# New constants for the order planner of a Mamba-2 plus routed-attention kernel

## The chip, the cores and the metric

The kernel runs on one core of one Trainium2 chip. The metric is the device time of one execution in microseconds. Three executions of the kernel before took 3627.47, 3632.01 and 3639.0 us, with a median of 3632.01 us.

## The reference

The input is `x`, 8 sequences of 1024 tokens with 512 features. After a layer norm it goes two ways, and both results are added to `x`:

```
xn = layernorm(x)
# way 1, Mamba-2: d_inner 1024, state 128, 16 heads of 64
u  = layernorm(xn) * ln_w + ln_b
z, xBC, dt = split(u @ in_proj_w.T)
xBC = silu(causal_conv4(xBC) + conv_b);  dt = softplus(dt + dt_bias)
y  = selective scan over the 1024 tokens with exp(-exp(A_log) * dt)
y  = (y + D * xs) * silu(z);  y = y / rms(y) * gamma
way1 = xn + y @ out_proj_w.T
# way 2, for each of 4 groups g and 8 sequences b: routed attention
queries    = top 512 tokens of xn @ w_qr[g]
key_values = top 256 tokens of xn @ w_kvr[g]
q = queries @ w_q[g].T;  k, v = split(key_values @ w_kv[g].T)   # 8 heads of 64
v = v * sigmoid(key/value logit);  one null key and null value join them
o = softmax(q k^T / 8) v;  o = (o @ w_out[g].T) * sigmoid(query logit)
way2 = mean of o over the groups that took the token, null_token where none did
out  = x + way1 + way2
```

Products are computed to nearly single precision by splitting each factor into a high and a low half-precision part, so that a product is three matrix multiplications.

## The kernel before

**Two halves.** The first half is the Mamba way. It runs over 16 blocks of 512 tokens, each of 4 chunks of 128 tokens. In it, `turn` is a DMA that transposes a normed chunk into `xhT` (L2287), and `gate` is a DMA that transposes the gated result of a chunk into `yT` (L2293), from which `proj` multiplies by the output weights (L1275). Between the halves the top tokens are found by a search over 32 bits.

The second half is the attention. It runs over 32 items, one for each group and sequence. An item has these parts on TensorE:

- *prepare*: `q` (4 steps of 12 matmuls, L1314), `k` (2 steps, L1329), `v` (2 steps, L1343). They read `xq` and `xk`, which 6 transposing DMAs `row` (L2371) fill from 6 gathers.
- *maxima*: `max` (16 steps, L1359), each followed on VectorE by `max_out` (L1826 and L1827), which takes the row maximum; then `shift_turn` (L1367) and `null_turn` (L1375).
- *heads*: `score` (8 steps, L1389 and L1390) and `value` (8 steps, L1406 to L1410). Between them ScalarE takes the exponential (`soft`, L2100) and its high half (`high_p`, L2106); GpSimd (`low_p`, L2238) and VectorE (`low_v`, L1861) each make half of the low part. After `value`, VectorE divides (`norm_o`, L1867 and L1870), ScalarE and GpSimd split the result (`o_high` L2112, `o_low` L2243).
- *finish*: two transposing DMAs `oturn` (L2394) fill `oT`, and `out` (4 steps of 12 matmuls, L1421) multiplies by the output weights. ScalarE scales (`res`, L2119) and GpSimd adds the rows to the output by an indirect DMA (`store`, L2232).

Each engine executes its instructions in a fixed order and waits on semaphores. SP issues all DMAs other than the indirect and the adding ones, so a DMA that waits holds back every later one on that queue. `rank` (L1764) is a VectorE step that counts places for the gathers of a later item.

**The planner.** The order is worked out in Python when the kernel is built, and it is the same in every execution. It is made in two stages.

1. `weave` (L188) writes a rough line of TensorE steps. The heads of item n are the main thread. At share s of it, a `Part(feed, start, end)` (L180) has been brought to the share `start + s * (end - start)` of its own steps. Beside the heads of item n lie prepare(n+1), maxima(n+1) and finish(n-1) (L847 to L851). `HEAD_START` (L49) is a pause ahead of the heads.
2. `Order` (L197) runs a model of the five engines over that line. Each step has an engine, a duration, the steps that it waits for, the PSUM banks that it takes with the steps that give them back, and `extra`, a time from the end of its issue to its result (for DMAs the landing). When TensorE is free, the model goes through the first `ahead` steps still in the line, takes the first one of each kind, and starts the first of those that has its inputs and banks (L294). The other engines start the ready step with the earliest latest-start (`latest`, L221). That time comes from the steps that follow; for a step that gives a bank back it is also no later than its matmul's end plus `keep` (L234).

The times that the model reaches are used only to sort the steps into each engine's order and to choose the banks. The instructions, their sizes and their waits are not touched by any constant of the planner, except which step's bank a matmul waits for.

`AHEAD_M` and no `keep` are used for the Mamba half (`arrange`, L434), `AHEAD` and `KEEP` for the attention (`arrange_items`, L611).

Of the kernel before, what the change touches and what calls it, by code (L numbers as in the profile page):

```python
# [38 lines left out]

FIRST_SLICES = 12  # L40
SLOP = 0.7
KEEP = 4.0
AHEAD, AHEAD_M = 12, 4
TURNS = CK * 3.45 + 15.23
TURN_ISSUE, TURN_LANDS, GATE_LANDS = 0.6, 4.0, 5.0
CONV_START, CONV_END = -0.05, 1.05
AHEAD_1, CONV_START_1 = (-0.06, 3.64), -0.25
BEHIND = 2
HEAD_START = 1.0  # L49
NSLOT = 4  # L50
ROW_ISSUE, ROW_LANDS = 0.6, 4.0
O_ISSUE, O_LANDS = 0.6, 5.0
NW = 4 * D
SC = 128
NSP = NW // SC
# [141 lines left out]
class Order:  # L197
# [13 lines left out]
    def add(self, engine, us, step, after=(), seats=(), extra=0.0):  # L211

        self.nodes[step] = (engine, us, [a for a in after if a], seats, extra)
        if engine == "PE":
            self.line.append(step)
# [229 lines left out]
def arrange_steps(order, line, late):  # L445
# [3 lines left out]
    def last(step):  # L449
        return step if step[1] >= 0 else None  # L450
# [85 lines left out]
    for ch in range(NCH):  # L536
        i = ch // CK
        add("SP", 0.5, ("bc_in", ch), [("cum_store", i), last(("intra", ch - 2)), last(("bc_in", ch - 1))], extra=10.0)
        free = [] if ch < 2 or ends(ch - 2) else [("xw", ch - 2)] if opens(ch - 2) else [("xw", ch - 2), ("decayed", ch - 2)]
        add("DVE", 0.25, ("dec_arg", ch), [("bc_in", ch), ("cum_copy", i)] + free)  # L540
        add("ACT", 0.45, ("dec", ch), [("dec_arg", ch)])
        for k in range(4):
            add("ACT", 1.26, (f"diff{k}", ch), [("dec", ch)])
        add("ACT", 1.91, ("decay", ch), [(f"diff{k}", ch) for k in range(4)])
        add("DVE", 0.28, ("gram_out", ch), [("gram", ch), last(("mask", ch - 1))])
        add("DVE", 2.6, ("mask", ch), [("decay", ch), ("gram_out", ch)])
        add("ACT", 0.25, ("open_b", ch), [("open", ch), state_before(ch)])
        add("DVE", 1.22, ("xdt", ch), [("open", ch), ("bias_get", len(PIECES) - 1), ("slice_low", len(PIECES) - 1), last(("intra", ch - 1))] + ([] if ends(ch - 1) else [("xw", ch - 1)]))
        add("DVE", 1.22, ("dxs", ch), [("open", ch), ("xdt", ch), ("bias_get", len(PIECES) - 1), ("slice_low", len(PIECES) - 1), last(("y2" if opens(ch - 1) else "y_skip", ch - 1))])
        if not ends(ch):  # L550
            add("POOL", 2.0, ("xw", ch), [("xdt", ch), ("dec", ch), state_before(ch)])
            if not opens(ch):
                add("POOL", 2.5, ("decayed", ch), [("dec", ch), ("state_out", ch - 1)] + ([] if opens(ch - 1) else [("inter", ch - 1)]))
                add("DVE", 1.22, ("state_out", ch), [("state", ch), ("decayed", ch), ("inter", ch)])
            else:
                add("DVE", 1.22, ("state_out", ch), [("state", ch), last(("inter", ch - 1))])
        for j in range(2):
            add("ACT", 0.59, ("z_tanh", ch, j), [("z", ch, j), ("wout_low", KI - 1), last(("yz", ch - 1))])
            add("DVE", 0.69, ("z_silu", ch, j), [("z_tanh", ch, j)])
        if opens(ch):  # L560
            add("DVE", 1.22, ("y2", ch), [("intra", ch), ("dxs", ch), ("wout_low", KI - 1), last(("y_low", ch - 1))])
        else:
            add("DVE", 1.22, ("y_in", ch), [("inter", ch), ("cum_exp", i), ("y_low", ch - 1)])
            add("POOL", 2.7, ("y_skip", ch), [("y_in", ch), ("dxs", ch)])
            add("DVE", 1.22, ("y2", ch), [("intra", ch), ("y_skip", ch)])
        add("DVE", 1.23, ("yz", ch), [("y2", ch), ("z_silu", ch, 0), ("z_silu", ch, 1)])
        add("ACT", 1.2, ("square", ch), [("yz", ch), last(("gate", ch - 1))])
        add("DVE", 0.2, ("mean", ch), [("square", ch)])
        add("POOL", 0.8, ("root", ch), [("mean", ch)])
        add("ACT", 1.15, ("y_high", ch), [("root", ch)])  # L570
        add("DVE", 1.4, ("y_low", ch), [("y_high", ch)])
        add("SP", TURN_ISSUE, ("gate", ch), [("y_low", ch), last(("proj", ch - 1))], extra=GATE_LANDS)
        add("ACT", 0.58, ("proj_out", ch), [("proj", ch), last(("o_add", ch - 2))])
        add("POOL", 1.0, ("o_add", ch), [("proj_out", ch), ("skip_store", i)], extra=5.0)
    if not late:
        return
    blk = NBLK - 1
    for h in range(2):
        add("DVE", 0.65, ("rank_get", h), [("rank_in", h), ("skip_store", blk)])
    for bit in range(31, -1, -1):  # L580
        add("DVE", 1.7, ("bit", bit), [("bit", bit + 1) if bit < 31 else ("rank_get", 1)])
    add("DVE", 0.9, ("ranks_zero", 0), [("inter", CK * blk - 1)])
# [28 lines left out]
def arrange_items(plan, line):  # L611
# [57 lines left out]
    for n in range(ITEMS):  # L669
        if n:  # L670
            for j in range(RT):
                if j in (0, QT):
                    add("SP", 0.5, ("rank_load", n, j // QT), [("rank", n, j - 1) if j else ("slot", n - 1)], extra=3.5)
                add("DVE", 1.05, ("rank", n, j), [("rank_load", n, j // QT), ("rank", n, j - 1) if j else ("slot", n - 1)])
            add("DVE", 0.2, ("slot", n), [("rank", n, RT - 1)] + each("store", n - NSLOT, QT) + each("qscore", n - 2, QT) + each("gather", n - 4, RT))
            for j in range(RT):
                add("POOL", 1.05, ("gather", n, j), [("slot", n), ("row", n - 1, RT - 1 if j >= QT else QT - 1)] + ([("row_score", n - 1, j)] if j >= QT else []), extra=4.0)
                read = ("q", n - 1, KD - 1) if j < QT else ("v", n - 1, KT - 1)
                add("SP", ROW_ISSUE, ("row", n, j), [("gather", n, j), read], extra=ROW_LANDS)
                if j >= QT:  # L680
                    add("DVE", 0.1, ("row_score", n, j), [("gather", n, j), ("v_low", n - 1, KT - 1)])
# [13 lines left out]
        if n % NB < 2:  # L695
            add("DVE", 1.2, ("keys_null", n), [("nulls", n // NB), ("max", n - 2, QT * H // 2 - 1)] + ([("keys_id", 1)] if n == 1 else []))
        for k in range(QT * H // 2):
            add("DVE", 0.84, ("max_out", n, k), [("max", n, k)] + [("null_arg", n - 1)])
        add("DVE", 0.3, ("shift", n), each("max_out", n, QT * H // 2) + [("shift_turn", n - 1), ("null_split", n - 1)])
        add("DVE", 0.25, ("null_arg", n), [("shift", n)])  # L700
        add("DVE", 0.42, ("shift_out", n), [("shift_turn", n), ("shift_in", n - 1)])
# [4 lines left out]
        for h in range(H):  # L706
            add("ACT", 1.05, ("soft", n, h), [("score", n, h), back_by("low_p", n, h, 2), back_by("low_v", n, h, 2)])
            add("ACT", 1.05, ("high_p", n, h), [("soft", n, h), back_by("value", n, h, LAG + 1)])
            add("POOL", 1.2, ("low_p", n, h), [("high_p", n, h)])
            add("DVE", 1.0, ("low_v", n, h), [("high_p", n, h)])  # L710
            add("DVE", 0.66, ("norm_o", n, h), [("value", n, h), back_by("o_low", n, h, 2)])
            add("ACT", 0.42, ("o_high", n, h), [("norm_o", n, h)] + each("oturn", n - 1, QT // 2))
            add("POOL", 0.7, ("o_low", n, h), [("o_high", n, h)])
# [10 lines left out]
def make_plan():  # L724
# [119 lines left out]
    for n in range(ITEMS):  # L844
        others = []
        if n + 1 < ITEMS:
            others.append(Part(Feed(prepare(n + 1), 20.8, record), 0.2, 2.0))  # L847
            others.append(Part(Feed(maxima(n + 1), 10.2, record), -0.7, 1.1))
        if n:
            others.append(Part(Feed(finish(n - 1), 10.4, record), -0.7, 1.2))  # L850
        weave(Feed(heads(n), HEAD_START + H * 1.8, record), *others)  # L851
    for gen in (last_values(), finish(ITEMS - 1)):
        Feed(gen, 1, record).to(1)
# [1615 lines left out]
```

## Time and profile before

| | us |
|---|---|
| median of three executions | 3632.01 |
| the profiled execution | 3642.05 |
| its span, first to last instruction | 3640.7 |
| TensorE busy | 3360.3 (92%) |
| VectorE busy | 2962.7 (81%) |
| ScalarE busy | 2273.6 (62%) |
| GpSimd busy | 1850.6 (51%) |

The mean granted clock of TensorE was 0.968 of full speed. Busy shares are means over the whole span; a busy time of TensorE is of pipelined matmuls, so an end-to-start overlap is counted once. A wait is put down to the engine whose signal came last.

### The profile page before, as it was taken

To read this page: it belongs to the slowest core of one execution; us is meant where nothing else is said; L and a number is where in the kernel's file an instruction comes from. 1 tells how busy PE (TensorE), PEld (TensorE's weight loads), DVE (VectorE), ACT (ScalarE), POOL (GpSimd) and SP (SyncE) were. 2 spreads that over 40 slices of the span, in tenths; PEclk is the share of its full clock that TensorE was granted. 3 is DMA by queue.
4 is the path that set the end of the run, shared out by engine and by line. 5 is a ranking of instruction groups with operands and counts; after the bars stand their busy time and mean duration, and the time that the engine had idled before them with its cause. 6 is when DMAs were issued, how large, how long until landed. Compare 5 with 4: busy or idle time off the path is not lost.

```text
span 3640.7 us, 64398 instructions
## 1 busy us (share of the span) xinstructions
PE 3360.3 (92%) x24312; PEld 1940.5 (53%) x24312; DVE 2962.7 (81%) x5336; ACT 2273.6 (62%) x4329; POOL 1850.6 (51%) x1483
## 2 busy tenths in 40 slices
PE   6899999999999999999748999999999999999997
PEld 4455555555555555555424555555555555555554
DVE  6798989999898988989967777787787877787774
ACT  5767767677767666776426555566555755555564
POOL 1332433334343332323437888877665765666565
PEclk9899999999999999999868999999999999999998
DMA  5444544465554445444387576777676676577664
GB/s 160 94 109 112 114 94 102 102 128 114 116 120 81 102 114 116 116 103 84 77 127 158 101 131 119 127 147 151 120 141 128 146 133 125 115 133 136 126 113 68
DMA packets 834213, 428.02 MB, mean 118 GB/s; under 512 B 575239, under 2 KB 758663, under 8 KB 831856
## 3 DMA queue, kind: packets, MB, share of 16 engines
q1 hardware_dynamic: 777584, 320.97, 42.5%
q0 software_dynamic: 56320, 102.94, 15.9%
q8 instruction: 193, 3.16, 0.4%
q14 instruction: 116, 0.95, 0.1%
HBM read 176.19 MB, written 101.71 MB: 76 GB/s over the span
## 4 chain that ended last, share of the span: by engine, by line
PE 58%; DVE 14%; DMA 8%; issue 5%; POOL 5%; ACT 4%; SPq 1%; another core or an unknown queue 0%; POOLq 0%; ACTq 0%; DVEq 0%
PE pair L1314 7%; PE pair L1275 7%; PE pair L1197 7%; PE pair L1421 7%; PE pair L1245 6%; PE pair L1285 4%; PE pair L1329 3%; DMA oT<-ohl 2%; PE pair L1343 2%; PE pair L1389 2%; PE pair L1390 2%; PE pair L1359 2%; PE pair L1256 2%; PE pair L1265 2%; DMA de<-cum 2%
## 5 line engine op out<-in xcount | busy, mean ns | idle before, releaser
L2238 POOL TENSOR_TENSOR ph<-pf,ph 128x512 f16<-128x512 f32 x256 | 354.8, 1386 | 243.8 <-ACT ph L2106 241.6
L1571 DVE SCALAR_TENSOR_TENSOR cv<-raw,taps,cv 128x512 f32<-128x512 f32 x480 | 428.6, 919 | 29.1 <-ACT cv L1978 27.9
L1826 DVE TENSOR_REDUCE smx<-pair 128x2 f32<-128x514 f32 x512 | 349.7, 684 | 88.3 <-PE pair L1359 85.5
L1197 PE MATMUL pair<-xhT,whi 128*128 128x512 f16 x1280 | 385.5, 383 | 8.1 <-ACT btok L1998 2.1
L2100 ACT ACTIVATE pf<-pair 128x1024 f32<-128x1024 f32 x256 | 261.6, 1023 | 155.0 <-PE pair L1390 131.8
L1275 PE MATMUL pair<-ohi,yT 128*128 128x512 f16 x1024 | 319.8, 384 | 27.1 <-DMA yT<-yhl 25.8
L1245 PE MATMUL pair<-zhi,xhT 128*128 128x512 f16 x1024 | 326.2, 380 | 1.5 <-ACT btok L1998 1.2
L1861 DVE TENSOR_TENSOR ph<-pf,ph 128x512 f16<-128x512 f32 x256 | 254.8, 995 | 84.3 <-ACT ph L2106 81.3
L2008 ACT ACTIVATE de<-de,cum 128x128 f32<-128x128 f32 x1024 | 309.5, 388 | 1.2
L2106 ACT CAST ph<-pf 128x1024 f16<-128x1024 f32 x256 | 267.3, 1044 | 4.9 <-PE pair L1410 0.2
L1285 PEld LDWEIGHTS pair<-xdt,de 128*128 128x128 f32 x2048 | 244.7, 196 | 20.4 <-issue 12.5
L2232 POOL DMA_INDIRECT y<-res,slot_i x128 | 208.4, 1628 | 84.9 <-ACT res L2119 65.9
L1285 PE MATMUL pair<-xdt,de 128*128 128x64 f32 x2048 | 242.7, 278 | 6.9 <-DVE dxs L1607 6.9
L2243 POOL TENSOR_TENSOR ohl<-of,ohl 128x256 f16<-128x256 f32 x256 | 202.8, 808 | 83.7 <-ACT ohl L2112 81.9
L1197 PE MATMUL pair<-xhT,wlo 128*128 128x512 f16 x640 | 245.1, 383 | 0.0
L1408 PE MATMUL pair<-vhi,ph 128*128 128x65 f16 x2048 | 243.8, 196 | 0.5 <-issue 0.5
L1410 PE MATMUL pair<-vhi,ph 128*128 128x65 f16 x2048 | 243.7, 195 | 0.3 <-issue 0.3
L1409 PE MATMUL pair<-vlo,ph 128*128 128x64 f16 x2048 | 243.3, 195 | 0.0
L2211 POOL DMA_INDIRECT gat<-rows,slot_i x192 | 197.4, 1028 | 55.6 <-issue 32.7
L1406 PE MATMUL pair<-nvb,pnT 96*128 96x65 f16 x1024 | 202.3, 198 | 21.3 <-issue 6.7
L2172 POOL TENSOR_TENSOR yn<-yn,neghalf 128x1 f32<-128x1 f32 x64 | 49.1, 767 | 335.4 <-DVE yn L1661 335.2
L1197 PEld LDWEIGHTS pair<-xhT,whi 128*128 128x128 f16 x1280 | 124.1, 99 | 169.6 <-issue 36.3
(260 smaller groups left out, 9811.6 us busy)
## 6 DMA issues: line engine op xcount, KB each, us to landing
de<-cum SPq DMA_DIRECT2D x64, 1024.0 KB, 9.4
rows<-rowt SPq DMA_DIRECT2D x16, 1040.0 KB, 6.2
xin<-x SPq DMA_DIRECT2D x16, 1024.0 KB, 8.8
y<-xin SPq DMA_DIRECT2D x16, 1024.0 KB, 5.7
y<-ob POOLq DMA_DIRECT2D x64, 256.0 KB, 4.6
qb<-qa SPq DMA_DIRECT2D x32, 512.0 KB
rbc<-rank SPq DMA_DIRECT2D x63, 256.0 KB
wst<-wkv SPq DMA_DIRECT2D x32, 256.0 KB
```

The source lines that it names most:

```text
L1197: ins = pe.matmul(bk[:], w[:, k, ws], xt[:, ha, k, :], start=n == 0, stop=n == 3 * KD - 1)
L1245: pe.matmul(pz[:], xt[:, ha, k, cs], w[:, k, j * 512:(j + 1) * 512], start=n == 0, stop=False)
L1275: ins = pe.matmul(bk[:], yT[:, ha * KI + k, :], w[:, k, :], start=k == 0 and n == 0, stop=k == KI - 1 and n == 2)
L1285: ins = pe.matmul(pw[:, h * HD:(h + 1) * HD], de[ch % 2][:, h, :], xdt[:, h, :], start=True, stop=True)
L1314: ins = pe.matmul(bk[:], w[:, k, ws], xq[:, ha * KD + k, :], start=n_ == 0, stop=n_ == 3 * KD - 1)
L1421: ins = pe.matmul(bk[:], o_[:, ha * KD + k, :], w[:, k, :], start=k == 0 and m == 0, stop=k == KD - 1 and m == 2)
L1571: ve.scalar_tensor_tensor(c_[:], r_[:, t:t + BLK], taps[:, ct, t:t + 1], c_[:], ALU.mult, ALU.add).then_inc(done, 1)
L1826: ve.tensor_reduce(smx[:, qt, 2 * h2:2 * h2 + 2], sc[:, :, 0:NK + 1], AX.X, ALU.max)
L2008: ins = ac.activation(d_[:, h, :], d_[:, h, :], ACT.Relu, bias=cum_t[i % 2][:, c, h:h + 1], scale=-1.0)
L2100: ac.activation(f[:].rearrange("p k q -> p (k q)"), bank("score", n, h)[:], ACT.Exp, scale=SCALE).then_inc(S.pf, 1)
L2106: ac.copy(p_[:, 0], f[:]).then_inc(S.ph, 1)
L2238: po.tensor_tensor(p_[:, 1, 1], f[:, 1], p_[:, 0, 1], ALU.subtract).then_inc(S.plp, 1)
```

## The change

No instruction is added or taken away. Constants of the planner change, and one dependency of its model is added. The durations and landing times that the model gives to the four kinds of transposing DMAs become longer in issue and shorter in landing. Three VectorE durations (`rank`, `max_out`, `low_v`) become shorter. `KEEP` goes from 4 to 6, `AHEAD` from 12 to 24, `HEAD_START` from 1.0 to 0.5, and the three parts beside the heads get other starts and ends. `TURN_ISSUE`, `TURN_LANDS`, `GATE_ISSUE` and `GATE_LANDS` are used in the Mamba half; all others act on the attention, `ROW_...` also on the first rows at the end of the Mamba half. `rank_get` 1 is now ordered behind `rank_get` 0.

```diff
-KEEP = 4.0
-AHEAD, AHEAD_M = 12, 4
+KEEP = 6.0
+AHEAD, AHEAD_M = 24, 4
-TURN_ISSUE, TURN_LANDS, GATE_LANDS = 0.6, 4.0, 5.0
+TURN_ISSUE, TURN_LANDS = 1.3, 2.5
+GATE_ISSUE, GATE_LANDS = 1.9, 2.9
-HEAD_START = 1.0
+HEAD_START = 0.5
-ROW_ISSUE, ROW_LANDS = 0.6, 4.0
-O_ISSUE, O_LANDS = 0.6, 5.0
+ROW_ISSUE, ROW_LANDS = 1.3, 2.7
+O_ISSUE, O_LANDS = 2.9, 2.6
...
-        add("SP", TURN_ISSUE, ("gate", ch), [("y_low", ch), last(("proj", ch - 1))], extra=GATE_LANDS)
+        add("SP", GATE_ISSUE, ("gate", ch), [("y_low", ch), last(("proj", ch - 1))], extra=GATE_LANDS)
...
-        add("DVE", 0.65, ("rank_get", h), [("rank_in", h), ("skip_store", blk)])
+        add("DVE", 0.65, ("rank_get", h), [("rank_in", h), ("skip_store", blk)] + ([("rank_get", h - 1)] if h else []))
...
-                add("DVE", 1.05, ("rank", n, j), ...
+                add("DVE", 0.95, ("rank", n, j), ...
-            add("DVE", 0.84, ("max_out", n, k), ...
+            add("DVE", 0.7, ("max_out", n, k), ...
-            add("DVE", 1.0, ("low_v", n, h), [("high_p", n, h)])
+            add("DVE", 0.85, ("low_v", n, h), [("high_p", n, h)])
...
-            others.append(Part(Feed(prepare(n + 1), 20.8, record), 0.2, 2.0))
-            others.append(Part(Feed(maxima(n + 1), 10.2, record), -0.7, 1.1))
+            others.append(Part(Feed(prepare(n + 1), 20.8, record), 0.1, 1.8))
+            others.append(Part(Feed(maxima(n + 1), 10.2, record), -0.5, 1.1))
         if n:
-            others.append(Part(Feed(finish(n - 1), 10.4, record), -0.7, 1.2))
+            others.append(Part(Feed(finish(n - 1), 10.4, record), -1.0, 1.3))
```

## Rows read from the trace of the kernel before

**Rows 1.** Busy time by stretch: length, engines, TensorE clock, DMA share, GB/s.
```profile
150.00:1740.00 1590.00, 1543.90 (x8620) 873.01 (x8619) 1429.27 (x1987) 1121.10 (x2569) 569.93 (x360) 0.99 0.49 107
1740.00:1900.00 160.00, 92.59 (x430) 50.72 (x430) 123.67 (x222) 55.16 (x107) 57.16 (x46) 0.76 0.58 94
1926.00:3582.00 1656.00, 1561.08 (x14301) 922.16 (x14300) 1274.29 (x2847) 970.30 (x1404) 1149.87 (x1017) 0.98 0.69 129
3582.00:3641.00 59.00, 40.31 (x354) 20.97 (x351) 13.92 (x26) 24.35 (x33) 32.69 (x27) 0.82 0.47 72
```

**Rows 2.** Timeline of TensorE: first score of the first and of the last item.
```profile
1925.70 0.38 PE L1389 MATMUL pair<-qa,ka 128*128 128x512 f16 x1
...
3581.89 0.61 PE L1389 MATMUL pair<-qa,ka 128*128 128x512 f16 x1
```

**Rows 3.** The same timeline, first scores of two neighbouring items.
```profile
2684.85 0.38 PE L1389 MATMUL pair<-qa,ka 128*128 128x512 f16 x1
...
2734.64 0.38 PE L1389 MATMUL pair<-qa,ka 128*128 128x512 f16 x1
```

**Rows 4.** Busy time of two items, one short and one long, columns as in rows 1.
```profile
2683.00:2733.00 50.00, 49.59 (x467) 29.85 (x465) 42.21 (x98) 30.28 (x44) 32.09 (x30) 1.00 0.71 135
...
3061.00:3120.00 59.00, 53.77 (x445) 30.08 (x442) 41.12 (x97) 29.77 (x43) 32.25 (x30) 0.91 0.61 114
```

**Rows 5.** Waits of TensorE from 1926 to 3582: total us, times, longest.
```profile
PE pair L1421 <- DMA oT<-ohl: 16.1, 11, 3.8
PE pair L1359 <- DVE snl L1827: 11.3, 14, 2.8
PE pair L1359 <- DVE of L1870: 8.9, 5, 2.2
PE pair L1375 <- DVE pnm L1850: 7.6, 5, 3.8
PE pair L1314 <- DVE of L1870: 7.0, 11, 1.8
...
PE pair L1359 <- ACT pf L2100: 4.9, 9, 0.9
PE pair L1406 <- DVE snl L1827: 4.6, 5, 1.8
PE pair L1314 <- DMA xq<-gat: 3.3, 2, 2.6
PE pair L1406 <- ACT pf L2100: 3.0, 4, 0.8
```

**Rows 6.** Waits of VectorE in the same stretch.
```profile
DVE rden L1867 <- remote: 20.7, 12, 3.0
```

**Rows 7.** Transposing DMAs by line: ns on SP's queue, min/median/max.
```profile
L2287 SPq DMA_TRANSPOSE xhT<-xh x64: 1232/1290/6423, 32.2 to 1601.5; - x64
...
L2293 SPq DMA_TRANSPOSE yT<-yhl x64: 1322/1932/4442, 133.3 to 1835.9; - x64
...
L2371 SPq DMA_TRANSPOSE xq<-gat x128: 1231/1302/3152, 1860.1 to 3516.0; - x128
...
L2394 SPq DMA_TRANSPOSE oT<-ohl x64: 1613/2949/4913, 1992.7 to 3618.7; - x64
```

**Rows 8.** Chain of waits: from a transpose's issue to its landing.
```profile
1835.94 4.29 DMA yT<-yhl
...
3616.62 4.50 DMA oT<-ohl
```

**Rows 9.** Timeline of SP's queue in a long item.
```profile
2912.92 2.81 SPq L2394 DMA_TRANSPOSE oT<-ohl  x1
2915.83 8.75 SPq L2371 DMA_TRANSPOSE xq<-gat  x2
2924.63 2.08 SPq L2394 DMA_TRANSPOSE oT<-ohl  x1
```

**Rows 10.** Timeline of VectorE: two `max_out` steps without a gap.
```profile
2616.92 0.68 DVE L1826 TENSOR_REDUCE smx<-pair 128x2 f32<-128x514 f32 x1
2617.52 0.14 DVE L1827 TENSOR_REDUCE snl<-pair 128x2 f32<-128x4 f32 x1
2617.59 0.68 DVE L1826 TENSOR_REDUCE smx<-pair 128x2 f32<-128x514 f32 x1
```

**Rows 11.** `low_v` from 1900 to the end: ns min/median/max; then its mean.
```profile
L1861 DVE TENSOR_TENSOR ph<-pf,ph x256: 669/693/3818, 1929.2 to 3609.9; 128x512 f16<-128x512 f32 x128
...
L1861 DVE TENSOR_TENSOR ph<-pf,ph 128x512 f16<-128x512 f32 x256 | 254.8, 995 | 84.3 <-ACT ph L2106 81.3
```

**Rows 12.** Waits of TensorE from 150 to 1700.
```profile
PE pair L1275 <- DMA yT<-yhl: 10.9, 4, 6.7
```

More of the change, by code:

```diff
@@ L673, in arrange_items @@
                     add("SP", 0.5, ("rank_load", n, j // QT), [("rank", n, j - 1) if j else ("slot", n - 1)], extra=3.5)
-                add("DVE", 1.05, ("rank", n, j), [("rank_load", n, j // QT), ("rank", n, j - 1) if j else ("slot", n - 1)])
+                add("DVE", 0.95, ("rank", n, j), [("rank_load", n, j // QT), ("rank", n, j - 1) if j else ("slot", n - 1)])
             add("DVE", 0.2, ("slot", n), [("rank", n, RT - 1)] + each("store", n - NSLOT, QT) + each("qscore", n - 2, QT) + each("gather", n - 4, RT))
@@ L697, in arrange_items @@
         for k in range(QT * H // 2):
-            add("DVE", 0.84, ("max_out", n, k), [("max", n, k)] + [("null_arg", n - 1)])
+            add("DVE", 0.7, ("max_out", n, k), [("max", n, k)] + [("null_arg", n - 1)])
         add("DVE", 0.3, ("shift", n), each("max_out", n, QT * H // 2) + [("shift_turn", n - 1), ("null_split", n - 1)])
```

## The prediction

> **What bounds the kernel now.** I read the busy times by stretch first [rows 1]. TensorE is busy 1543.9 of 1590 us in the Mamba half, so at most 46 us are idle there, and 1561.1 of 1656 us in the attention from the first score of item 0 to that of item 31, where 95 us are idle. So TensorE bounds both halves, and an order can only take idle time away. Between the halves (1740 to 1900) 67 us are idle, and 19 us in the tail, but these hang on chains of dependent steps.
>
> Next, the items one by one on TensorE's timeline. From the first score of item 0 to that of item 31 there are 3581.89 - 1925.70 = 1656.2 us for 31 items [rows 2], 53.4 us each. But the items differ: one lasts 2734.64 - 2684.85 = 49.8 us [rows 3] with 49.6 of 50 us busy at a clock of 1.00, another some 59 us with 53.8 busy at 0.91 [rows 4]. The work is the same. If all took 49.8 us, 31 x 3.6 = 112 us would go. That is the ceiling of this change in the attention. It has two parts. 95 us are idle. The rest is the clock: a mean of 0.98 between the two levels 1.2 and 2.4 GHz means that about 4% of the 1656 us, 66 us, ran at the lower level and did 33 us of work. So each idle microsecond drags 33 / 95 = 0.35 us of clock along.
>
> Then the waits of TensorE in that stretch [rows 5]. The largest single one is for `oT`, 16.1 us in 11 waits. Those for `xq` add 3.3. The others are for VectorE and ScalarE, mostly to give a PSUM bank back: 11.3 + 8.9 + 7.6 + 7.0 + 4.9 + 4.6 + 3.0 = 47.3 us in the rows shown.
>
> **The change part by part.** No instruction comes or goes, so every microsecond must come from waits.
>
> *DMA constants.* The medians on SP's queue are 1.29 us for `turn`, 1.93 for `gate`, 1.30 for `row`, 2.95 for `oturn` [rows 7]. The model had 0.6 for all; it gets 1.3, 1.9, 1.3, 2.9. An item has 6 `row` and 2 `oturn` steps, so the model held the queue for 8 x 0.6 = 4.8 us where the chip needs 6 x 1.3 + 2 x 2.9 = 13.6 us. Issue plus landing was 5.6 for `oturn` and becomes 5.5, for `gate` 5.6 and becomes 4.8; one of each measured 4.50 and 4.29 [rows 8]. So a lone transpose was never late. A pair was: the model let the second `oturn` follow after 0.6 us. In the worst item the second was issued 2924.63 - 2912.92 = 11.7 us after the first, because two `row` transposes lay between them [rows 9]. A model that knows this should put `oturn` ahead of rows that nobody needs yet, and `out` later. The start of `finish` in the weave also moves, from share 0.7/1.9 = 0.37 of the heads to 1.0/2.3 = 0.43, which is later by 0.06 x 50 = 3 us. Bounds: nothing gained (the rows 3.3 and 16.1 stay) to 19.4 us gained. Against this, some transposes take up to 4.9 us, which no constant covers. I take two thirds, -13 us.
>
> *VectorE constants.* `max_out` is two instructions of 0.68 and 0.15, but in a run of them the next starts 0.67 us after the first [rows 10], so 0.7 is nearer than 0.84; 16 of them free 2.2 us per item in the model. `low_v` has a median of 0.693 and a mean of 0.995 [rows 11], so 0.85 lies between and is too short for the mean; that adds 8 x 0.15 = 1.2 us of hidden load. Together with `rank` (6 x 0.1) the model's VectorE loses 4.0 us per item, with the engine busy 1274.3 / 1656 = 77%. Where the model said that TensorE had to wait for `max_out`, it now packs closer.
>
> *Longer view and weave.* With 12 steps of view a run of `max` steps, of which 16 follow each other, can fill the view, and the next item's `q` isn't seen. With 24 it is. The long items have their stalls just there: TensorE has only `max` and `score` left, and they wait for banks. Maxima now begin at share 0.5/1.6 = 0.31 and not 0.39, and prepare ends at 0.9/1.7 = 0.53 and not 0.44, so `q`, `k` and `v` last longer as filling. For both edits together the bounds are +47 us (as much again as the 47.3 us of waits shown) and -47 us. But 20.7 us of VectorE's waits in `norm_o` come from something outside the order [rows 6], in 12 waits of up to 3.0 us, and TensorE's waits for `of` hang on those. I take a quarter off, -12 us.
>
> *KEEP.* Steps that give a bank back may start 2 us later in the ranking. That is a cost, and the only edit that must be one where banks are short. Its bounds are 0 and one microsecond for each item, 31 us. I take +8, nearer zero since TensorE's longest waits for a bank, 2.8 and 2.2 us, are few.
>
> *Clock.* Idle time falls by 13 + 12 - 8 = 17 us, and 0.35 x 17 gives -6 us. The chip lowers the clock in the items with stalls: 0.91 in the long item and 1.00 in the short one [rows 4]. The Trainium skill, "TensorE: Matmul & The Clock Gate", section "A second HAM failure mode: psum-queue depth-cycling", says that frequent small idle times between groups of matmuls, as PSUM banks go round, are enough to lower the clock. The trace agrees, since no wait of [rows 5] is over 3.8 us and the clock still falls. By that rule a change that only removes the `oT` waits and leaves the bank waits would give no clock back, and the sum would be 6 us smaller.
>
> *Mamba half.* Here only `turn` and `gate` change. SP is mostly waiting there, so 0.7 and 1.3 us more of queue cost nothing in themselves. Waits for `yT` are 10.9 us in 4 [rows 12]. Both steps get a latest start 0.8 us later, which puts `low` and `y_low` behind other VectorE work; that engine is 90% busy there [rows 1], and it is what hides or bares it. Bounds -11 and +15 us (a quarter of a microsecond for each of 64 chunks); I take -2. `rank_get` is two steps and changes nothing. Entry and tail of the attention: 0, bounds 5 either way.
>
> Sum: -13 - 12 + 8 - 6 - 2 = -25 us. The profiled execution took 3642.05 us (span 3640.7 and 1.35 around it), so 3617. It lay 10.0 us over the median 3632.01, and the forecast for the median is **3607 us**. Its own range is 3585 to 3621.
>
> **The rivals.** About 0.3%, 11 us, is what a measurement of this kernel can tell from no change, so faster means under 3621 and slower over 3643.
>
> - *Banks come back late.* Place: `max_out`, `soft`, `norm_o` and `res` on VectorE and ScalarE, pushed behind other ready work by `KEEP` 6, by a `low_v` priced 0.15 too low and by `max` packed at 0.7. For it: the bank waits are already the largest sort [rows 5], and VectorE does its work in bursts. Against it: the model itself sees banks, and fits TensorE's order to them. Price: 1 us more for each of 31 items, 31, and the clock on it 11, less the 13 + 5 from the transposes and 2 of Mamba: +22, so 3654. It decides once the seven waits of 47.3 us pass 47.3 + 18 = 65 us.
> - *The stalls only move.* The items fall out of step because `row`, `gather` and VectorE's outside waits shift from item to item, and each order meets them somewhere; or the view of 24 seldom finds anything new. Then the `oT` gain turns into waits for `xq` or banks. 3632, within 9 either way. For it: the same work takes 49.8 us in one item and 59 in another [rows 3, 4], although each has the same parts in its weave.
> - *Most items become short ones.* The model now holds the queue rightly, and half of the 112 us goes: 3632 - 56 = 3576. For it: an item reaches 49.8 us already with the wrong constants [rows 3]. Against it: the 20.7 us of [rows 6] and slow transposes stay.
>
> **How the numbers follow.** Chances: forecast 0.42, banks late 0.22, only moved 0.19, most items short 0.17. Faster: 0.38 of the forecast, all of the last, 0.02 of the third: 0.57. Slower: 0.20 of the second and 0.01 of the third: 0.21. The same: 0.22. The range of 8 in 10 is 3565 to 3655: it takes in the middle of the last rival and of the first, and leaves out about a tenth on each side.
>
> **What would show it.** Right: the wait for `oT` falls from 16.1 to about 5 us and `xq` stays small; TensorE's idle time in the attention falls from 95 to about 78 us; the mean item goes from 53.4 towards 52.7 us; the clock of that stretch goes from 0.98 towards 0.985; the Mamba stretch keeps 1590 within some 10 us. Wrong: waits of L1359, L1406 and L1314 for VectorE and ScalarE that grow past 65 us, or waits for `xq` or `oT` as large as before, or a Mamba half that is longer by over 10 us.

## The result and the profile after

The kernel after takes 3649.82 us (median of 4, 3646.82 to 3658.36) beside 3632.32 us (median of 4) for the kernel before in the same comparison. The ratio is 1.0051 with a 95% interval of 1.0027 to 1.0075. It is slower, by 17.5 us; the forecast was 25 us faster. The time lies inside the range given (3565 to 3655), on the wrong side of no change. In the experiments' first comparison one execution of the kernel before took 9113.62 us at a granted clock of 0.557; it is in the median given for it below and in no ratio.

The two traces differ by less than the medians. The profiled execution of before lay 9.7 us over its median of this comparison and that of after 3.0 us under its own, so the spans are 3640.7 and 3645.5 us. The traces have to account for 4.8 us, and what they show is where waits moved, not the whole 17.5 us.

Busy time of the kernel after by stretch, columns as in [rows 1]:

```profile
150.00:1740.00 1590.00, 1536.68 (x8527) 866.60 (x8526) 1424.05 (x1971) 1105.30 (x2539) 577.94 (x355) 0.99 0.48 106
1740.00:1900.00 160.00, 99.43 (x499) 54.90 (x497) 127.96 (x216) 61.47 (x127) 57.93 (x44) 0.81 0.59 91
1924.00:3589.00 1665.00, 1563.10 (x14309) 919.53 (x14310) 1306.76 (x2860) 986.79 (x1414) 1144.57 (x1019) 0.99 0.74 129
3589.00:3646.00 57.00, 38.61 (x380) 20.64 (x378) 15.09 (x27) 24.49 (x33) 34.96 (x30) 0.89 0.49 75
```

The third line is the attention. TensorE is idle there for 1665.0 - 1563.1 = 101.9 us, where it was 94.9. In the first line TensorE has done 7.2 us less of the Mamba work by 1740 us and catches up in the second. Timeline of TensorE, first score of the first and of the last item, as in [rows 2]:

```profile
1924.32 0.58 PE L1390 MATMUL pair<-qa,ka 128*128 128x512 f16 x1 [2.58 <-issue]
...
3588.83 0.38 PE L1390 MATMUL pair<-qa,ka 128*128 128x512 f16 x1 [0.75 <-issue]
```

That is 1664.5 us for 31 items, 53.7 each, against 1656.2: +8.3 us. The attention begins 1.4 us earlier and the tail is 2.1 us shorter, which leaves the 4.8 us. Waits of TensorE in the kernel after, from 1924 to 3589 (lines are one higher than in [rows 5]):

```profile
PE pair L1376 <- DVE pnm L1851: 21.3, 22, 1.7
PE pair L1390 <- DVE snl L1828: 15.6, 14, 2.8
PE pair L1360 <- DVE snl L1828: 14.5, 27, 1.5
PE pair L1360 <- DMA ka<-ka: 11.2, 12, 2.2
PE pair L1407 <- DVE snl L1828: 9.3, 19, 1.6
...
PE pair L1422 <- DMA oT<-ohl: 6.5, 4, 2.9
...
PE pair L1315 <- DMA xq<-gat: 2.3, 2, 2.0
...
PE pair L1360 <- DVE of L1871: 0.2, 1, 0.2
```

The wait for `oT` fell from 16.1 to 6.5 us, and those for `of` from 8.9 + 7.0 to 0.2. In their place the waits for `snl`, the second half of `max_out`, went from 18.2 us (the 11.3 and 4.6 of [rows 5] and 2.3 more) to 15.6 + 14.5 + 9.3 = 39.4, those for `pnm` from 7.6 to 21.3, and waits for `ka`, the doubled keys, came in with 11.2. Smaller rows fell: those for `pf` from 8.9 to 2.5, for `res` from 4.1 to 1.4. So the waits for VectorE's maxima are now the largest, with those for `pnm` behind them. What VectorE itself waited for, same stretch:

```profile
DVE rjunk L1765 <- DMA rbc<-rank: 49.7, 30, 7.0
```

and in the kernel before, from 1926 to 3582:

```profile
DVE rjunk L1764 <- DMA rbc<-rank: 10.5, 13, 2.7
```

`rjunk` is the output of the `rank` step, and `rbc` its input, loaded by SP (`rank_load`). The model prices that load at 0.5 us of queue and 3.5 us more to its landing, 4.0 from issue to landing. `rank` stands in VectorE's fixed order, so while it waits, every `max_out` behind it waits too, and with it a PSUM bank. One such place, on SP's queue of the kernel after:

```profile
3079.99 3.98 SPq L2395 DMA_TRANSPOSE oT<-ohl  x1
3084.07 0.54 SPq L2359 DMA_DIRECT2D rbc<-rank  x1
```

and in its chain of waits, start and length:

```profile
3084.07 6.51 DMA rbc<-rank
3090.60 0.89 DVE rjunk L1765 x2
...
3093.99 0.61 DVE smx L1827
...
3094.73 0.40 PE pair L1360 x2
```

The load leaves late because `oturn` holds the queue for 3.98 us, it lands after 6.51 us and not 4.0, then come `rank` steps, a maximum, and only then TensorE. This is a long case: from 2000 to 3560 us the load took 3.2, 4.4 and 7.5 us (least, median, most), so at the median the price was 0.4 us too short. This gave the theory for the experiments: **R**, the edits make VectorE's modelled order tighter around `rank`, whose load the model prices too short. Its rivals stand in the expectations, in numbers.

### The profile page after: what moved, and what is told of

Same layout as the page of the kernel before. It is cut to its first block, busy times and chain, and to the rows that moved or that the text cites. A ratio compares the mean times of both kernels' runs of the same rounds, so it can differ in the third digit from the quotient of the medians.

```text
span 3645.5 us, 64376 instructions
## 1 busy us (share of the span) xinstructions
PE 3354.3 (92%) x24312; PEld 1932.9 (53%) x24312; DVE 2996.9 (82%) x5336; ACT 2281.6 (63%) x4329; POOL 1858.9 (51%) x1483
## 3 DMA queue, kind: packets, MB, share of 16 engines
q0 software_dynamic: 56320, 102.94, 16.1%
## 4 chain that ended last, share of the span: by engine, by line
PE 22%; DVE 11%; DMA 8%; POOL 6%; issue 4%; ACT 1%; SPq 1%; DVEq 0%; ACTq 0%; POOLq 0%
PE pair L1315 5%; PE pair L1422 4%; PE pair L1330 3%; DMA oT<-ohl 2%; DVE smx L1827 2%; DMA gat<-rows,slot_i 2%; DVE ph L1862 2%; DMA rbc<-rank 2%; PE pair L1344 2%; PE pair L1390 2%; PE pair L1391 2%; POOL ph L2239 1%; PE pair L1360 1%; DVE rjunk L1765 1%; DVE pnm L1848 1%
## 5 line engine op out<-in xcount | busy, mean ns | idle before, releaser
L2239 POOL TENSOR_TENSOR ph<-pf,ph 128x512 f16<-128x512 f32 x256 | 345.2, 1356 | 186.7 <-ACT ph L2107 184.1
L2244 POOL TENSOR_TENSOR ohl<-of,ohl 128x256 f16<-128x256 f32 x256 | 210.5, 833 | 87.1 <-ACT ohl L2113 85.6
L2113 ACT CAST ohl<-of 128x256 f16<-128x256 f32 x256 | 100.6, 402 | 244.8 <-DVE of L1871 132.2
L1765 DVE TENSOR_SCALAR_CACHE_REDUCE rjunk<-rbc,cst 128x640 f16<-128x640 f16 (+1 forms) x190 | 182.4, 960 | 63.2 <-DMA rbc<-rank 61.7
```

Of the source, the lines that this page charges most:

```text
L2239: po.tensor_tensor(p_[:, 1, 1], f[:, 1], p_[:, 0, 1], ALU.subtract).then_inc(S.plp, 1)
```

## The experiments

Each ratio is to the kernel before on the same chip. There were five comparisons: e1 to e4, e5 to e8, e9 to e12, e13 to e16, e17 and e18. The medians of the kernel before in them were 3642.53, 3625.86, 3629.22, 3622.27 and 3622.23 us. Waits are those of one profile each, between 1926 and 3560 us unless a row says otherwise.

### Which half, and which group of edits

**e1: the Mamba edits alone.**

```diff
-TURN_ISSUE, TURN_LANDS, GATE_LANDS = 0.6, 4.0, 5.0
+TURN_ISSUE, TURN_LANDS = 1.3, 2.5
+GATE_ISSUE, GATE_LANDS = 1.9, 2.9
...
+ ([("rank_get", h - 1)] if h else [])
```

> The kernel before with only the Mamba edits (the turn and gate constants, the rank_get dependency). My forecast had -2 us for them. The trace after has its last proj matmul of the Mamba half 7.5 us later than before. Theory M (the shorter landing times let VectorE do y_low and low later, and TensorE waits for yT and xhT): the half is 7 us longer, the whole is slower by 5 to 9 us, ratio 1.0015 to 1.0025. Rival N (the 7.5 us are one execution's chance, and the attention has all of the loss): within 2 us of before.

Measured 1.0018 (0.9998 to 1.0037).

**e2: all but those.** The edit is the whole change with the lines of e1 taken back.

> The kernel before with all edits but the Mamba ones. Theory M leaves about 10 of the 17.5 us of the whole change here: ratio 1.002 to 1.004. Rival N: all 17.5 us here, 1.005. My forecast's own sum would be -23 us, 0.994.

Measured 1.0063 (1.0040 to 1.0087), 3664.0 us. The loss is in the attention's constants. Taking the Mamba edits away did not make it smaller.

**e3: the weave alone.**

```diff
-HEAD_START = 1.0
+HEAD_START = 0.5
...
-  prepare 0.2, 2.0   maxima -0.7, 1.1   finish -0.7, 1.2
+  prepare 0.1, 1.8   maxima -0.5, 1.1   finish -1.0, 1.3
```

> The kernel before with only the weave edits: HEAD_START 0.5 and the new starts and ends of the three parts. Theory W (maxima start earlier in the line, so max meets the landing of the doubled keys and null_turn its split): waits of L1359 for ka and of L1375 for pnm appear as in the trace after (11 and 21 us), and the kernel is slower by 5 to 15 us. Rival V (VectorE's short durations do it): no change within 5 us here, the waits as before.

Measured 1.0150 (1.0123 to 1.0176).

**e4: the three VectorE durations alone.**

```diff
-rank 1.05   max_out 0.84   low_v 1.0
+rank 0.95   max_out 0.7    low_v 0.85
```

> The kernel before with only the VectorE durations shortened (rank 0.95, max_out 0.7, low_v 0.85). Rival V (4 us of load per item hidden from the model, max packed closer than VectorE can follow): waits of TensorE for snl and of, 24.8 us before, rise past 35 us, slower by 8 to 20 us. Theory W: within 5 us of before, or faster, since 0.7 is what a run of max_out shows.

Measured 1.0110 (1.0083 to 1.0137). The two traces lose in different places. TensorE in e3:

```profile
PE pair L1421 <- DMA oT<-ohl: 39.8, 19, 5.6
PE pair L1367 <- DVE shift L1832: 18.7, 11, 2.1
PE pair L1359 <- DVE snl L1827: 15.7, 22, 2.3
```

and in e4:

```profile
PE pair L1359 <- DVE snl L1827: 38.4, 30, 2.9
PE pair L1367 <- DVE shift L1832: 17.6, 15, 2.9
PE pair L1421 <- DMA oT<-ohl: 11.1, 13, 2.1
```

They share two things. One is VectorE's wait for the rank load, 79.3 us in e3 and 58.8 in e4, where before has 10.5. The other is TensorE's wait for `shift`, the VectorE step behind the last `max_out` of an item, where before has 2.3. And the parts do not add: 1.5% and 1.1% alone, 0.6% with everything else.

The orders that the planner writes show where the first comes from. Of the 31 items with a rank load for the query tokens (kind 0), it stands on SP directly behind an `oturn` in 0 in the kernel before, 8 in e4, 22 in e3 and 27 in after. On VectorE, the first `rank` stands on average 3.6 steps behind the `slot` of the item before, in before and after alike. So VectorE's order around this `rank` did not get tighter, as R has it. What changed is the place of the load on SP.

**e5: a nudge of no meaning.** `res` priced 0.72 for 0.7, in the kernel before.

```diff
-            add("ACT", 0.7, ("res", n, qt), ...
+            add("ACT", 0.72, ("res", n, qt), ...
```

> The kernel before with one harmless nudge of the planner: ScalarE's res step is priced 0.72 instead of 0.70 us. Nothing real is truer or less true. Theory S (the kernel before sits on a lucky order, and any other order of about the same quality is slower): ratio 1.002 to 1.012, as for the other edits. Rival T (only what the edits say counts): within 3 us, ratio 0.999 to 1.001.

Measured 0.9997 (0.9979 to 1.0015). So this other order is not slower by being another. Its waits differ all the same: `oT` 6.6 us and `snl` 25.4, where before has 16.1 and 18.2. Differences of that size in one row say little about the time.

**e6: KEEP alone.**

```diff
-KEEP = 4.0
+KEEP = 6.0
```

> The kernel before with only KEEP 6. My slower rival of the prediction (banks come back late): waits of TensorE on VectorE and ScalarE grow past 65 us, slower by over 20 us. Theory S: slower by 5 to 40 us, but with waits of any sort and not of the banks above all. Theory T without the bank rival: within 5 us.

Measured 0.9985 (0.9967 to 1.0002). The waits for `snl` rise to 24.5 + 6.2 + 3.8 = 34.5 us, yet no time is lost. So waits of that size are not by themselves a slower kernel.

**e7: the measured `row` and `oturn` alone.**

```diff
-ROW_ISSUE, ROW_LANDS = 0.6, 4.0
-O_ISSUE, O_LANDS = 0.6, 5.0
+ROW_ISSUE, ROW_LANDS = 1.3, 2.7
+O_ISSUE, O_LANDS = 2.9, 2.6
```

> The kernel before with only the attention's transposing DMAs priced as measured (ROW 1.3 and 2.7, O 2.9 and 2.6). My forecast's first term: waits for oT from 16.1 to about 5 us, faster by 13 us and the clock on it, ratio 0.995. Theory S: slower by 5 to 40 us, whatever the wait for oT does.

Measured 1.0021 (1.0005 to 1.0038). TensorE in e7:

```profile
PE pair L1421 <- DMA oT<-ohl: 21.9, 13, 4.0
...
PE pair L1314 <- DMA xq<-gat: 10.1, 3, 5.2
```

The wait that these constants were to mend grew from 16.1 us, and that for `xq` from 3.3. The profiled execution lay 17.6 us over its median, so these rows can be above the usual.

### The price of the rank load

**e8: the kernel after, with the landing of `rank_load` priced 8.0.**

```diff
-  add("SP", 0.5, ("rank_load", n, j // QT), ..., extra=3.5)
+  add("SP", 0.5, ("rank_load", n, j // QT), ..., extra=8.0)
```

> The kernel after with the landing of the rank load priced 8.0 instead of 3.5 us, so that the planner puts the rank steps later in VectorE's order. Theory R (VectorE stands 50 us at rank steps whose load is queued on SP behind the transposes, and the row maxima behind them reach TensorE late): the wait of VectorE for rbc falls from 50 to below 15 us, the waits of TensorE for snl from 39 to below 25, and the kernel is 10 to 25 us faster than after, ratio to before 0.998 to 1.002. Rival (VectorE has slack and the rank wait is cover): the wait for rbc falls, the time stays at 1.005.

Measured 1.0006 (0.9993 to 1.0019). VectorE's wait for the load is no longer among its waits. TensorE in e8:

```profile
PE pair L1407 <- ACT pf L2101: 16.9, 25, 0.8
PE pair L1376 <- DVE pnm L1851: 13.3, 10, 2.7
PE pair L1422 <- DMA oT<-ohl: 12.6, 8, 5.7
PE pair L1360 <- DVE snl L1828: 8.3, 14, 1.3
...
PE pair L1390 <- DVE snl L1828: 6.9, 5, 1.9
```

The waits for `snl` are 16.3 us with a third row of 1.1, where after has 39.4. Part of that came back elsewhere: those for `pf` on ScalarE rose from 2.5 to 16.9 us, and `oT` from 6.5 to 12.6. What the price does to VectorE's order is seen on its timeline. In the kernel after, where the first `rank` comes 2930.49 - 2923.79 = 6.7 us behind the `slot` of the item before, it finds the load not there, and two follow each other:

```profile
2923.79 0.15 DVE L1775 SCALAR_TENSOR_TENSOR slot_i<-slot_f,cst 128x6 int32<-128x6 f32 x1
...
2930.49 0.88 DVE L1765 TENSOR_SCALAR_CACHE_REDUCE rjunk<-rbc,cst 128x640 f16<-128x640 f16 x1 [0.82 <-DMA rbc<-rank]
...
2931.41 0.88 DVE L1765 TENSOR_SCALAR_CACHE_REDUCE rjunk<-rbc,cst 128x640 f16<-128x640 f16 x1
```

and in e8, where it comes 11.4 us behind, with three maxima before it:

```profile
2918.32 0.15 DVE L1775 SCALAR_TENSOR_TENSOR slot_i<-slot_f,cst 128x6 int32<-128x6 f32 x1
...
2929.71 0.87 DVE L1765 TENSOR_SCALAR_CACHE_REDUCE rjunk<-rbc,cst 128x640 f16<-128x640 f16 x1
```

On average the first `rank` now stands 8.1 steps behind `slot`, where after has 3.6. On SP the load still stands directly behind an `oturn` in 25 items. So the price acts on VectorE's order and not on the load's place.

The same edit was then put on each part.

**e9: the weave with 8.0** (edits of e3 and e8).

> Only the weave edits, and the rank load's landing priced 8.0 instead of 3.5. The weave alone had the largest wait of VectorE for rbc (79 us) and 1.015. Theory R: that wait falls below 15 us and most of the loss goes, ratio below 1.006. Rival O (the weave loses by its waits for oT, 40 us): rbc falls, the ratio stays above 1.010.

Measured 1.0115 (1.0092 to 1.0137). It mends little. VectorE still waits 22.4 us for the load, where under 15 was expected, and TensorE 24.0 us for `oT` and 16.2 for `shift`. The expectation's rival, a loss that stays above 1.010, came true.

**e10: the VectorE durations with 8.0** (e4 and e8).

> Only the shorter VectorE durations, and the rank load's landing priced 8.0. The durations alone had a wait for rbc of 59 us and 1.011. Theory R: rbc below 15 us, ratio below 1.004. Rival V (the hidden load packs max too close): the waits of TensorE for snl stay near 50 us and the ratio stays above 1.008.

Measured 1.0007 (0.9989 to 1.0025), where e4 had 1.0110. TensorE in e10:

```profile
PE pair L1359 <- DVE snl L1827: 12.3, 16, 1.8
```

All rows for `snl` are 23.6 us, where e4 has 50.2, and `shift` fell from 17.6 to 0.9. VectorE waits for no rank load. But e4's profile also has 35.7 us of VectorE's outside waits (the `remote` of [rows 6]) and e10's has none. The two ran on different chips, so a part of this difference may be the chip's.

**e11: all but Mamba with 8.0** (e2 and e8).

> All edits but the Mamba ones, and the rank load's landing priced 8.0: the changed kernel mended in the attention and without its 6 us in the Mamba half. Theory R with theory M: 0.9985 to 1.000, and faster than the same with the Mamba edits (1.0006). If it stands above 1.003, the two causes don't add up.

Measured 0.9987 (0.9969 to 1.0004), 3623.15 beside 3629.22 us; e2 had 1.0063. Here too the outside waits before `rden` differ: 34.7 us in e2's profile, none in e11's.

**e12: the kernel before with 8.0.**

> The kernel before with the rank load's landing priced 8.0 and nothing else. Its wait for rbc is only 10.5 us, so theory R gives it at most that: ratio 0.997 to 1.000. If it gains as much as the changed kernel did (0.4% or more), the price of 8.0 helps by another way than the rank wait; if it loses by over 0.3%, the order matters more than the rank steps.

Measured 1.0033 (1.0017 to 1.0048). The price alone is no gain; it costs a third of a per cent. TensorE in e12:

```profile
PE pair L1314 <- DMA xq<-gat: 19.4, 7, 4.3
```

Before has 3.3 there. A later `rank` makes a later gather, and `q` waits for its rows. So e8, e10 and e11 did not come out well by a gain that was there for the kernel before too.

**e14: weave, `row` and `oturn`, and 8.0** (e3, e7 and e8).

> The weave edits with the measured ROW and O prices, and the rank load priced 8.0. The weave with the rank load at 8.0 alone has 1.0115 and waits for oT of 24 us. If the later finish needs the true price of the oturn pair (my forecast's first term), oT falls below 15 us and the ratio below 1.007. If the weave is bad in itself with the old VectorE durations, it stays above 1.009.

Measured 1.0031 (1.0014 to 1.0049), against 1.0115 for e9. The measured transposes cost 0.2% alone (e7) and give 0.8% back here. They do not do it by the wait for `oT`, which is 20.6 us beside 24.0 in e9 and was expected under 15. What fell from e9 is the wait for `shift`, 16.2 us, which is no longer among TensorE's, and VectorE's wait for the rank load, from 22.4 us to nothing. The waits for `pf` rose from 18.7 to 31.4.

**e15: KEEP, the VectorE durations and 8.0** (e6, e4 and e8).

> KEEP 6, the shorter VectorE durations and the rank load priced 8.0; old weave, old transposes, old Mamba constants. A try at a version that beats both kernels. If the parts add up (0.9985 and 1.0007): 0.998 to 1.000. The spread of orders makes anything from 0.996 to 1.004 no surprise.

Measured 0.9991 (0.9976 to 1.0007), 3617.13 beside 3622.27 us.

### Taking the wait away in the order after

If the wait for the load were itself the cost, an order that differs from after in that wait only should win.

**e13: in the kernel after, VectorE's `rank` steps stand four steps later in its own list**, never past the `slot` step that needs them.

```diff
-            for step in plan:
+            for step in later([step for step in plan if step[0] in does]):
...
+                    if step[0] == "rank" and step[1] > 1:
+                        held.append([by, step])
```

> The kernel after, with every engine's order as it is but VectorE's, in which each rank step stands four steps later (never behind its slot step). Theory R, direct: the wait of VectorE for rbc falls from 50 to below 25 us, what stood behind it comes earlier, and the ratio to before falls from 1.005 to 1.000 to 1.003. Rival O (the other orders made the difference in the run with the load priced 8.0, since SP, TensorE and banks moved too): ratio stays at 1.004 to 1.007.

Measured 1.0171 (1.0146 to 1.0197). VectorE's wait for the load is gone, and TensorE's for `snl` went up to 87 us:

```profile
PE pair L1360 <- DVE snl L1828: 52.0, 45, 2.2
PE pair L1390 <- DVE snl L1828: 22.2, 19, 3.4
...
PE pair L1407 <- DVE snl L1828: 12.8, 21, 0.8
```

SP, whose next load waits for the last `rank`, in e13 (its L2375 is L2359 of after) and then in after:

```profile
SPq L2375 <- DVE rjunk L1765: 132.3, 29, 11.4
```

```profile
SPq L2359 <- DVE rjunk L1765: 30.1, 18, 3.7
...
SPq L2359 <- DVE slot_i L1775: 5.5, 4, 2.5
```

**e17: in the kernel after, a `rank_load` right behind an `oturn` stands ahead of it on SP** (27 of 31 places).

```diff
+                    if step[0] == "rank_load" and step[2] == 0 and out[-1][0] == "oturn":
+                        out.insert(len(out) - 1, step)
```

> The kernel after with one change of order on SP alone: where the rank load of kind 0 stands right behind an oturn transpose (27 of 31 items), the two change places. All other engines' orders, and the banks, are as in after. Theory R, direct and without the SP stall that e13 brought: the load lands some 4 us earlier, VectorE's wait for rbc falls from 50 to below 20 us, TensorE's waits for snl from 39 to below 25, ratio from 1.005 to 1.000 to 1.003. Rival (the wait is cover, VectorE has nothing urgent behind it): rbc falls, snl and the ratio stay.

Measured 1.0335 (1.0309 to 1.0362). VectorE's wait fell from 49.7 to 16.5 us. TensorE and SP in e17:

```profile
PE pair L1422 <- DMA oT<-ohl: 106.5, 25, 9.0
```

```profile
SPq L2359 <- DVE rjunk L1765: 112.4, 25, 8.6
SPq L2359 <- DVE slot_i L1775: 104.2, 28, 6.8
```

The two rows of SP were 30.1 and 5.5 us in after. The load was last on SP for a reason: it waits for the `slot` of the item before. Moved ahead, it stops SP with the transposes behind it, and `oT` waits 106.5 us. Both runs refute the simple form of R, that the wait for the load can be lifted out by itself. What they fit is a chain of `slot`, load, `rank` and the next `slot` with little slack in it, whose delay shows on VectorE, on SP or on TensorE; no run took the chain itself apart.

### The Mamba half

**e16: `gate` 1.9 and 2.9 alone.**

```diff
-TURN_ISSUE, TURN_LANDS, GATE_LANDS = 0.6, 4.0, 5.0
+TURN_ISSUE, TURN_LANDS = 0.6, 4.0
+GATE_ISSUE, GATE_LANDS = 1.9, 2.9
```

> The kernel before with only gate priced 1.9 and 2.9 (turn stays at 0.6 and 4.0). Theory M for the gate: y_low runs later behind other VectorE work, the waits for yT grow, the last proj matmul of the Mamba half starts at about 1855 us as in the three runs with all Mamba edits, against a mean of 1850 without; ratio about 1.0015. If turn has the loss: 1850 and 1.000.

Measured 1.0018 (1.0003 to 1.0032).

**e18: `turn` 1.3 and 2.5 alone.**

```diff
-TURN_ISSUE, TURN_LANDS, GATE_LANDS = 0.6, 4.0, 5.0
+TURN_ISSUE, TURN_LANDS = 1.3, 2.5
+GATE_ISSUE, GATE_LANDS = 0.6, 5.0
```

> The kernel before with only turn priced 1.3 and 2.5 (gate stays at 0.6 and 5.0). With gate alone the last proj matmul of the Mamba half started at 1845.6 us, no later than before. If turn has the loss: about 1855 and ratio 1.002. If neither alone has it: 1846 to 1851 and 1.000, and the loss comes only from both together.

Measured 1.0029 (1.0015 to 1.0042). The last `proj` of the Mamba half starts at 1845.6 us in e16 and at 1842.0 in e18. With both constants it starts at 1855.0 (after), 1854.4 (e1), 1855.8 (e8), 1851.2 (e13) and 1856.6 (e17), on average 1854.6. In the 13 profiles with the old Mamba constants it starts between 1844.8 and 1855.7, on average 1850.2. Those 13 have one and the same order in this half, so the 10.9 us between them are scatter. So both together may make the half some 4 us longer, and in one profile each neither constant alone does. e16 missed its 1855 us and had its ratio of about 1.0015; e18 met neither of its two cases. As to the time, two pairs of kernels have the same order in the attention and differ in the Mamba edits alone. They contradict each other: 1.0051 with them (after) and 1.0063 without (e2), 1.0006 with (e8) and 0.9987 without (e11). The Mamba edits cost between -0.1% and +0.2%, and the runs do not settle it. The attention's order also changes in e1, e16 and e18, although none of its constants did. It is the same new order in all three, and no other kernel has it. So their 1.0018, 1.0018 and 1.0029 can be the price of that order as well as of the Mamba half.

## Why the prediction was wrong

**DMA constants and transposes, -13 us.** The sign shown for it came true: `oT` fell by 9.6 us, `xq` stayed small with 2.3. That is luck as far as the runs show, since the nudge of e5 has 6.6 us for `oT` too. The cause given did not hold. Alone (e7) the constants raised `oT` to 21.9 us and cost 0.2%. They did not bring the pair together either. In the kernel before, `row` steps stand between the two `oturn` steps in 29 of 32 items; in e7 it is still 29, and in after 1. The planner gives 2 with the weave and the VectorE durations alone, without any new transpose price. The constants went with a faster kernel only in an order with the new weave (e14 against e9).

Nor was the price true where it was used. On SP's queue `oturn` went from a median of 2.949 us in before [rows 7] to 4.007 in after:

```profile
L2395 SPq DMA_TRANSPOSE oT<-ohl x64: 1925/4007/6340, 1996.3 to 3623.3; - x64
```

From issue to landing it took 4.7, 6.2 and 8.9 us (least, median, most, 2000 to 3560 us), where the model has 5.5. The prediction's "a lone transpose was never late" rested on one landing of 4.50 us in the tail. A duration measured in one order was not the duration in the order made from it.

**VectorE constants, longer view and weave, -12 us.** This is the step that failed. It argued that with truer durations and more filling TensorE packs closer, and took a quarter of the bank waits off: from 47.3 us to 35. The same seven waits came to 47.8, and with the row of L1390, which stood outside the seven, from 49.6 to 63.4. Measured, the waits for `snl` rose by 21.2 us and for `pnm` by 13.7, and `ka` came in with 11.2. Alone, the VectorE durations cost 1.1% (e4) and the weave 1.5% (e3). The reading of [rows 10] was right, and that was not the point. The old 0.84 and 1.05 were too long for their own steps. The runs fit that they left room for the rank load, which came late: with it at 8.0 the loss of e4 is gone (e10), though on another chip. The longer view did nothing: given the other edits, `AHEAD` 24 and 12 give the same order, step for step. In the kernel before by itself it would change the order, and that was not run.

**KEEP, +8 us.** Wrong in sign or in size: 0.9985 with an interval up to 1.0002 (e6). The bank wait was to be paid in full, but 34.5 us of waits for `snl` in e6 cost nothing, since TensorE waited less elsewhere: its waits of all sorts from 1926 to 3560 us are 76.2 us in e6 and 89.3 in before.

**Clock, -6 us.** The granted clock of the attention went from 0.98 to 0.99 although idle time rose by 7 us. The pairing of idle time with clock by 0.35 does not hold. By the rule of the Trainium skill ("TensorE: Matmul & The Clock Gate", "A second HAM failure mode: psum-queue depth-cycling"), that frequent small idle times between groups of matmuls as PSUM banks go round can lower the clock, more bank waits should if anything lower it. This trace does not show that. The longest waits are shorter now, 2.9 us where [rows 5] have 3.8; that this is the reason was not tested.

**Mamba half, -2 us.** The last `proj` starts 7.7 us later (1855.0 for 1847.3), inside the bounds of -11 and +15, on the other side of the value taken. The scatter of that start, 10.9 us in one order, is larger. `yT` waits 13.9 us where [rows 12] have 10.9:

```profile
PE pair L1276 <- DMA yT<-yhl: 13.9, 4, 6.8
```

**The outside waits of [rows 6].** They were taken as something that stays. The trace of after has none, nor have those of e5 to e18; before and e1 to e4 have them (10.6 to 35.7 us). e1 to e4 ran on one chip. So they seem to belong to an execution or a chip; they are largest in e2 and e4, and whether the order has a part in them was not tested. The fall of the `of` waits can come from that, so it is no proof of a better order.

**The rivals.** The time is nearest to *banks come back late* (3654, measured 3649.82), but its mark did not come. The seven waits of 47.3 us are 14.5 + 0.2 + 21.3 + 9.3 us in the rows above and 2.5 us for `pf`, together 47.8; with the 15.6 of L1390, which was 2.3, they are 63.4, under the 65. `KEEP`, its main cause, costs nothing by itself (e6); `low_v` priced too low was not run alone. What may stand is "`max` packed at 0.7", one of the three edits of e4, but what it collides with, the rank load, stood in none of the rivals. I had read VectorE's outside wait but not its 10.5 us for `rbc`, since it was small. *The stalls only move* describes the trace well: `oT` and `of` give 25 us, `snl`, `pnm` and `ka` take 46, and some 12 us came back in smaller rows, so that idle time rose by only 7.

**What is shown and what is open.** Shown: the loss is in the attention's constants (e2), both the weave (e3) and the VectorE durations (e4) lose alone, and their costs do not add. The kernels with the rank load priced later are rid of most of the loss for the VectorE durations (e4, e10) and for all of the attention's edits, with either Mamba half (e2 and e11, after and e8; these have one and the same pair of attention orders). It is not so for the weave (e3, e9) unless the transposes are priced longer too (e14), and the price costs something in the kernel before (e12). Only e12 was timed against its partner itself; the other pairs ran on different chips, each against the kernel before there, and a share of the chip's own in the ratios can't be excluded, above all in e2 and e4 with their outside waits. After and e8, whose profiles both have none, differ by 0.45% with intervals apart. Shown as well: lifting out the wait itself is no cure (e13, e17). Open: by which single wait the price acts; why the weave alone costs 1.5%; the Mamba half. The best versions, e11 and e15, are clearly faster than the kernel after (their intervals end at 1.0004 and 1.0007, after's begins at 1.0027), and not shown to be faster than the kernel before.

## What to carry to other kernels

In a planner of fixed orders a constant is not a measurement of its step alone: a price that is too long can be the slack for another that is too short. Before making one truer, look for the steps on the *other* engine's queue that have no slack (here `rank_load`, 4.0 us from issue to landing in the model, 4.4 at the median and 6.51 in a long case). See where the new order puts them on their queue, and time each edit alone and with the rest. Then measure the prices again in the new order, as `oturn` shows. Moving a waiting step by hand made the kernel slower both times here (e13, e17), since steps behind it on a queue then waited too.

## What the runs showed of the hardware

- The same `oturn` transpose held SP's queue for 2.949 us at the median and 4.913 at most in the kernel before [rows 7], and for 4.007 and 6.340 us in the kernel after. The transposes are the same in both, and the order is another. In e2, which has the attention's order of after, the median is 3.968, and in e5 it is 2.996. What beside it makes it longer was not tested.
- A gather took 3.4, 6.4 and 11.8 us from issue to landing (least, median, most) in the kernel after, from 2000 to 3560 us; the rank load 3.2, 4.4 and 7.5 us.
- `low_v` on VectorE takes 0.693 us at the median and 0.995 on average, up to 3.8 us [rows 11]. The Trainium skill, "SBUF — State Buffer", section "Who interferes with whom", says that a VectorE instruction with two inputs in SBUF and a GpSimd one that reads SBUF get in each other's way; the traces agree. In the kernel before, 190 of 255 `low_v` steps between 1930 and 3610 us overlap a two-input GpSimd instruction, and they take 1.10 us on average, 85 of them over 0.8; the other 65 take 0.69, the longest 0.77. In the kernel after it is 187 of 254 with 1.13 us, and 67 with 0.68 and at most 0.72.
